# Quantised feed-forward on one core: block powers applied to clipped values, inverse by one integer operation, Silu and gated product 1024 wide

## The reference

```python
def _quantize_elem(x, ebits, mfrac, max_norm):
    ax = jnp.abs(x)
    priv = jnp.floor(jnp.log2(jnp.where(ax == 0, 1.0, ax)))
    priv = jnp.maximum(priv, float(-2 ** (ebits - 1) + 2))
    scale = jnp.exp2(priv - mfrac)
    return jnp.clip(jnp.round(x / scale) * scale, -max_norm, max_norm)

def _quantize_mx(x, ebits, mfrac, emax_elem, max_norm):     # blocks of 32 along the last axis
    amax = jnp.max(jnp.abs(xb), axis=-1, keepdims=True)
    sexp = jnp.floor(jnp.log2(jnp.where(amax == 0, 1.0, amax))) - emax_elem
    scale = jnp.exp2(jnp.clip(sexp, -127.0, 127.0))
    return _quantize_elem(xb / scale, ebits, mfrac, max_norm) * scale

def _mx_linear(x, w):                                       # activations: (2, 3, 2, 7.5); weights: (2, 1, 2, 6)
    return jnp.einsum('bsh,oh->bso', _q_act(x), _q_w(w))

inter = jax.nn.silu(_mx_linear(y, w_gate)) * _mx_linear(y, w_up)    # y = layernorm(x), 256 -> 1024
x = x + _mx_linear(inter, w_down)                                   # 1024 -> 256
```

## Time and profile before

| | |
|---|---|
| median of 3 runs | 835.02 us |
| lowest, highest | 833.01, 839.99 us |
| span of the profiled execution (first to last instruction) | 832.7 us |
| time of the profiled execution outside its span | not given; the lowest run is 0.3 above the span |
| feed-forward stage in the profile | from about 742 us to the end |
| busy over the span: PE, DVE, POOL, ACT | 90%, 74%, 69%, 49% |
| granted PE clock over the span | 0.986 of full speed |

### The profile page before, as it was taken

One profiled execution on the slowest core, in us unless ns is written; L12 is line 12 of the kernel. 1 busy time (PEld: TensorE's weight loads), 2 busy tenths in 40 slices (PEclk: granted clock), 3 DMA queues, 4 the chain that ended last, 5 costly groups with the idle time before them and its releaser, 6 DMA issues. The chain is left out here.

```text
span 832.7 us, 14911 instructions
## 1 busy us (share of the span) xinstructions
PE 750.6 (90%) x4808; PEld 535.8 (64%) x4808; DVE 615.8 (74%) x1115; ACT 406.6 (49%) x1084; POOL 570.9 (69%) x589
## 2 busy tenths in 40 slices
PE   4999999859999999689999999999999999866785
PEld 2555555447878877556777777777777777543454
DVE  5898999868887878665565576886678667749995
ACT  1688888533322322216454544555454445444453
POOL 5667776326676757564657778787878887716976
PEclk9999999989999999999999999999999999998999
DMA  9200000040000010122110000000000000000011
GB/s 262 103 1 0 0 0 1 2 168 20 20 19 20 19 57 0 57 95 96 48 49 1 1 1 1 3 1 1 1 1 2 1 2 1 1 2 7 25 33 38
DMA packets 8763, 24.12 MB, mean 29 GB/s; under 512 B 1711, under 2 KB 5167, under 8 KB 8087
## 3 DMA queue, kind: packets, MB, share of 16 engines
q1 hardware_dynamic: 8154, 23.28, 8.5%
q10 hardware_dynamic: 549, 0.08, 0.1%
HBM read 21.26 MB, written 2.10 MB: 28 GB/s over the span
## 5 line engine op out<-in xcount | busy, mean ns | idle before, releaser
L1606 POOL TENSOR_TENSOR q<-turned 64x512 f32<-64x512 f32 x128 | 168.0, 1313 | 23.5 <-DVE turned L1532 9.5
L1283 PE MATMUL ps<-l_yt,a 128*128 128x512 f32 x576 | 144.1, 400 | 2.1 <-ACT p L1429 1.6
L1283 PEld LDWEIGHTS ps<-l_yt,a 128*128 128x128 f32 x576 | 104.9, 188 | 26.9 <-issue 4.7
L1593 POOL TENSOR_TENSOR p<-p,l_inverse 128x512 f32<-128x512 f32 x64 | 66.8, 1047 | 77.3 <-DVE l_inverse L1554 76.9
L1429 ACT ACTIVATE p<-ps,l_negmax 128x128 f32<-128x128 f32 x256 | 91.1, 382 | 43.1 <-DVE l_negmax L1523 43.1
L1532 DVE TENSOR_TENSOR turned<-ps,rope 128x1024 f32<-128x1024 f32 x64 | 78.0, 1220 | 42.4 <-PE ps L1283 39.8
L871 PE MATMUL ps<-yt_experts,wsplit 128*128 (+1 forms) x384 | 97.3, 403 | 5.7 <-DVE h L974 5.2
L467 DVE TENSOR_REDUCE negmax<-ps 128x4 f32<-128x512 f32 x128 | 84.4, 685 | 13.3 <-PE ps L290 12.8
L871 PEld LDWEIGHTS ps<-yt_experts,wsplit 128*128 128x128 f32 x384 | 71.2, 192 | 23.1 <-issue 5.4
L1523 DVE TENSOR_REDUCE l_negmax<-ps 128x4 f32<-128x512 f32 x64 | 41.2, 686 | 45.8 <-PE ps L1341 45.6
L383 ACT ACTIVATE pt<-ps 128x512 f32<-128x512 f32 x128 | 71.2, 599 | 6.8 <-PE ps L312 4.5
(11 more groups left out here) (213 smaller groups left out, 1571.1 us busy)
## 6 DMA issues: line engine op xcount, KB each, us to landing
wide<-in_wide SPq DMA_DIRECT2D x8, 768.0 KB, 4.5
mx_raw<-in_mx SPq DMA_DIRECT2D x8, 384.0 KB, 3.1
x<-in_x SPq DMA_DIRECT2D x4, 512.0 KB, 8.4
ctx_t<-in_ctx_t SPq DMA_DIRECT2D x1, 2048.0 KB, 7.8
out<-x SPq DMA_DIRECT2D x16, 128.0 KB, 1.7
narrow<-in_narrow SPq DMA_DIRECT2D x8, 192.0 KB, 2.7
ktraw<-in_ctx_rows SPq DMA_DIRECT2D x1, 1248.0 KB
wraw<-in_gate SPq DMA_DIRECT2D x1, 1024.0 KB, 18.1
```

The source lines that it names most:

```text
L1283: out = pe.matmul(tile_bank(n, k), a[i][:, pa, kin, k * 128:(k + 1) * 128], yt[j % 2][:, py, kin, :, :].rearrange("p b s -> p (b s)"), sta ...
L1593: pool.tensor_tensor(p[:, head, :, :], p[:, head, :, :], spread(inverse[:, head, :], 2, S), ALU.mult).then_inc(normed[head], 1)
L1606: t = pool.tensor_tensor(out[rows[(head + half) % 2], head, :], turned[rows[head], half, :], turned[rows[head], 2 + half, :], ALU.add)
```

## The change

The block power that multiplies the clipped values is now the masked exponent itself, written straight to `hscale` in SBUF (L1913 of the changed kernel). Before it was 16 times that; the factor 16 (`PART`) moves to ACT's last copy of the down product (L1888), and the residual's identity is divided by 16 in a tensor of its own (`ident_part`, made once by POOL, L2005). The inverse is computed from the same bits by one integer operation, 250 x 2^23 minus the bits (L1914), in place of a scaling with a floor and a reciprocal. Silu and the gated product are one instruction of 1024 columns each, over two banks (L1872, L1899); `gated` is one buffer of 1024 in place of two of 512. PE makes the whole gate, then the whole up projection: gate waits for the Silu of the sequence before, up for its product.

```diff
-        gated = [sb(f"f_gated{i}", [S, 512]) for i in range(2)]
+        gated = sb("f_gated", [S, FFN])
...
+        ident_part = sb("f_ident_part", [128, 128])
-        gate_ps, up_ps = [m.ps[:, 0, :], m.ps[:, 2, :]], [m.ps[:, 1, :], m.ps[:, 3, :]]
+        gate_ps, up_ps = (m.ps[:, 2 * i:2 * i + 2, :].rearrange("s c n -> s (c n)") for i in range(2))
...
+        PART = 0.25 / UNIT
+        H_STEPS, INVERSE = 3, 250
...
-                    for half in range(2):
-                        wait(pe, h_made[half], n)
-                        for i, (bank, made) in enumerate(((gate_ps[half], gate_made[half]), (up_ps[half], up_made[half]))):
+                    for i, (banks, made, free) in enumerate(((gate_ps, gate_made, gated_made), (up_ps, up_made, h_made))):
+                        wait(pe, free, n)
+                        for half in range(2):
                             for k in range(HALVES):
                                 c = k * FFN + half * 512
-                                t = pe.matmul(bank, f.yqt[:, n, k * S:(k + 1) * S], m.wq[:, i, c:c + 512],
-                                              start=(k == 0), stop=(k == 1))
-                            t.then_inc(made, 1)
+                                t = pe.matmul(banks[:, half * 512:(half + 1) * 512], f.yqt[:, n, k * S:(k + 1) * S],
+                                              m.wq[:, i, c:c + 512], start=(k == 0), stop=(k == 1))
+                        t.then_inc(made, 1)
...
-                    pe.matmul(down_ps[par], m.ident[:, :], m.x[:, n - 4, :], start=True, stop=False)
+                    pe.matmul(down_ps[par], ident_part[:, :], m.x[:, n - 4, :], start=True, stop=False)
...
-                    for half in range(2):
-                        act.wait_ge(gate_made[half], n + 1)
-                        wait(act, h_made[half], n)
-                        act.activation(gated[half][:, :], gate_ps[half], ACT.Silu).then_inc(gated_made[half], 1)
+                    act.wait_ge(gate_made, n + 1)
+                    wait(act, h_made, n)
+                    act.activation(gated[:, :], gate_ps, ACT.Silu).then_inc(gated_made, 1)
...
-                    act.activation(m.x[:, n - 4, :], down_ps[par], ACT.Copy).then_inc(x_made, 1)
+                    act.activation(m.x[:, n - 4, :], down_ps[par], ACT.Copy, scale=PART).then_inc(x_made, 1)
...
-                dve.tensor_tensor(h[par][:, half * 512:(half + 1) * 512], gated[half][:, :], up_ps[half],
-                                  ALU.mult).then_inc(h_made[half], 1)
+                dve.tensor_tensor(h[par][:, :], gated[:, :], up_ps, ALU.mult).then_inc(h_made, 1)
...
-                then(2, dve.tensor_scalar(hmax[par].bitcast(U32), hmax[par].bitcast(U32), EXPONENT, None, ALU.bitwise_and))
                 wait(dve, hq_made, n - 3)
-                then(3, dve.tensor_scalar(hscale[place][:, :], hmax[par], 0.25 / UNIT, 2.0 ** -122 / UNIT,
-                                          ALU.mult, ALU.max))
-                then(4, dve.reciprocal(hinverse[par][:, :], hscale[place][:, :]))
+                bits = hscale[place][:, :].bitcast(U32)
+                then(2, dve.tensor_scalar(bits, hmax[par].bitcast(U32), EXPONENT, None, ALU.bitwise_and))
+                then(3, dve.tensor_scalar(hinverse[par][:, :].bitcast(U32), bits, -1.0, float(INVERSE << 23),
+                                          ALU.mult, ALU.add))
...
-                    combine(n, par, 0)
-                    combine(n, par, 1)
-                    dve.wait_ge(h_made[0], n + 1)
-                    dve.wait_ge(h_made[1], n + 1)
+                    combine(n, par)
+                    dve.wait_ge(h_made, n + 1)
...
+            pool.tensor_scalar(ident_part[:, :], m.ident[:, :], 1.0 / PART, None, ALU.mult).then_inc(part_made, 1)
             steps(pool, body)
```

More of the change, by code:

```diff
@@ L1783, in feed_forward @@
         half_ps = [h_ps[:, 0:512], m.bank(0).bitcast(BF16)[:, 0:512]]
-        gate_made, up_made, gated_made, h_made = (
-            [sem(f"f_{n}{i}") for i in range(2)] for n in ("gate_made", "up_made", "gated_made", "h_made"))
+        PART = 0.25 / UNIT
+        H_STEPS, INVERSE = 3, 250
+        gate_made, up_made, gated_made, h_made, part_made = (
+            sem(f"f_{n}") for n in ("gate_made", "up_made", "gated_made", "h_made", "part_made"))
         h_step, h8_made, hc_made, hq_made, hq_turned, hq_kept = (
@@ L1826, in body @@
                         pe.wait_ge(f.x_mid, GROUPS)
+                        pe.wait_ge(part_made, 1)
                     if n - 4 < B - 1:
@@ L1850, in turn_last @@
                 pe.wait_ge(hq_kept, B - 1)
-                pe.wait_ge(h_made[0], B)
+                pe.wait_ge(gated_made, B)
                 for half in range(2):
@@ L1890, in _, with combine @@
         def _(dve):
-            def combine(n, par, half):
-                dve.wait_ge(gated_made[half], n + 1)
-                dve.wait_ge(up_made[half], n + 1)
+            def combine(n, par):
+                dve.wait_ge(gated_made, n + 1)
+                dve.wait_ge(up_made, n + 1)
                 wait(dve, h8_made, n - 1)
-                dve.tensor_tensor(h[par][:, half * 512:(half + 1) * 512], gated[half][:, :], up_ps[half],
-                                  ALU.mult).then_inc(h_made[half], 1)
+                dve.tensor_tensor(h[par][:, :], gated[:, :], up_ps, ALU.mult).then_inc(h_made, 1)
             def scales_of_h(n, place):
@@ L1902, in then @@
                     instruction.then_inc(h_step, 1)
-                    dve.wait_ge(h_step, SCALE_STEPS * n + k)
+                    dve.wait_ge(h_step, H_STEPS * n + k)
                 par = place % 2
@@ L1981, in body @@
                 if inside(n, B):
-                    pool.wait_ge(h_step, SCALE_STEPS * (n + 1))
+                    pool.wait_ge(h_step, H_STEPS * (n + 1))
                     wait(pool, hc_made, n - 1)
```

## The result

| | before | after |
|---|---|---|
| median of 22 runs each | 833.88 us | 830.48 us |
| lowest, highest | 832.43, 844.25 | 827.94, 836.92 |
| span of the profiled execution | 832.7 | 828.5 |

The ratio of after to before is 0.9943, with a 95% interval of 0.9922 to 0.9963. That is 4.8 us of 833.9, and 3.1 to 6.5 by the interval; the two medians by themselves are 3.4 apart. Forecast were 4.8 less and a time of 830.2. The profiled execution of the changed kernel took 830.3 for a span of 828.5, so 1.8 lie outside its span. So about 0.3 of the gain lies where the profile doesn't show it, and comes with the wide form. The prediction had no term for it, and why it is so was not looked into.

A forecast was written before the change was run, and what follows sets the result against it. DVE, never idle in an undisturbed feed-forward step of 4.63, was taken as the bound. Steps 7.95 plus start 0.15 less holds 3.32 gave 4.78 saved: 835.0 - 4.8 = 830.2 us, range 825.8 to 835.0.

The forecast's parts named there:

- DVE sets the pace and POOL idles 0.85: Undisturbed feed-forward step of 4.63: DVE is never idle, POOL is free 3.86 after inverse ready and idles 0.85.
- Wide product, 0.13 a step: Gated product as one 1024-wide instruction: 0.06 saved by the merge, 0.07 by one wait less (0.06 to 0.13).
- Scales, 0.40 a step: Mask, scaling and reciprocal, 0.82 together, become two 32-wide instructions of 0.42 on DVE, saving 0.40 a step.
- The slow integer form: Integer inverse on DVE as slow as the reciprocal (0.35): 0.16 less saved a step, 2.4 less gain.
- Two holds: Steps 5 and 7: integer inverse held by POOL's third instruction to about 5.76, costing 1.66 each, 3.32 together.
- rival A: Integer inverse is not held, as its margin against POOL's third instruction is only 0.09: 827.4, chance 0.20.
- Start, 0.15 gained: Start of the feed-forward stage: with one-piece Silu the first inverse is ready at 747.22 against 747.37, gain 0.15.
- The rest at nothing: Single Silu buffer, whole-width waits, ACT's scaling, scaled identity, POOL's extra instruction cost nothing; Silu ready 0.2 early at group transposes.
- the 15 steps: Feed-forward stretch from first inverse ready to POOL's last divide; 7.95 saved over 15 intervals, less 3.32.
- B: PE at its low clock after waiting needs 7.3 a step and becomes the bound; 846.2, chance 0.07.
- the sign of B: In the changed profile, PE's granted clock below 1 after 775 was to mean B.
- C's closed ring: Single buffers close the ring of product, Silu and PE's queue at the old 4.63: 838.2, chance 0.07.

The follow-up runs named there:

- wide_only: Changed kernel with scales and reciprocal as before, so only Silu and gated product are 1024 wide; 833.32 us, ratio to before 0.9971, the 15 steps 71.48.
- scales_only: Kernel before with only the new scales, integer inverse and factor 16 in the last copy; 830.93 us, ratio to before 0.9935, the 15 steps 70.32.
- extra_psum: psum_const plus one full-width POOL product into an unread scratch tile at step 2; 835.96 us (1 run), the 15 steps 66.24.
- psum_const: Changed kernel with the integer inverse as scalar-tensor-tensor, adding a constant tile in PSUM; 827.65 us, ratio to before 0.9915, the 15 steps 65.81.
- pool_pause: Changed kernel plus a 1-wide POOL addition ahead of the last group's divide and its multiply; 828.28 us, ratio to before 0.9914, the 15 steps 67.40.
- after_again: Changed kernel profiled and timed again, no edit; 831.55 us, ratio to before 0.9941, the 15 steps 68.57.

## Why the prediction was right

Step by step, as it put them.

- DVE sets the pace and POOL idles 0.85: right. With DVE faster POOL's gap shrank to 0.31, and DVE still set the pace in every undisturbed step.
- Wide product, 0.13 a step: 0.135 by itself. Of the bounds, 0.06 to 0.13, the upper one held, since the gap of 0.10 did fall to 0.03. The reason given, one wait less, is not shown (see wide_only). The product itself went from 1.28 to 1.22, so the merge saved 0.06. The prediction's estimate by the Trainium skill (VectorE: DVE Perf Modes, The DRAIN you can't avoid, and the page's formula for a tensor-tensor instruction) was 0.16 for it, and the runs don't agree; the row was the better guide.
- Scales, 0.40 a step: scales_only shows 4.63 to 4.22, 0.41; the integer instruction is 0.18, not 0.19. The slow integer form, bound at 0.35, didn't come.
- Two holds, ending 5.76 after the inverse before: 5.77 and 5.77. At 4.09 undisturbed each costs 1.68; 1.66 was forecast. The margin of 0.09 that rival A turned on was 0.08 (769.31 to 769.39).
- Start, 0.15 gained: 0.14.
- The rest at nothing: Silu is 1.02 and hidden. At step 10 it is ready 0.06 ahead of the product (790.50 + 1.03 against 791.59) in the changed kernel, where I had 0.2. It cost nothing here and 0.32 in extra_psum.

The sum over the 15 steps: 15 x 0.54 = 8.10, less 2 x 1.68 = 3.36, and 0.20 for the interval of 4.83 in the profile before; together 4.94, and 4.95 was measured. Forecast were 4.63 for this part. No term of the sum was off by more than 0.15 over the 15 steps, and the missing 0.3 are 0.01 a step and that one interval, which the sum took for an undisturbed one.

The whole came out at 4.2 in the profiled spans and 3.1 to 6.5 in the runs. The closeness of the 830.48 to 830.2 is partly luck. The forecast started from 835.02, a median of 3 runs; that of 22 runs is 833.88, from which 4.8 less would be 829.1. And several parts that nobody forecast are as large as the terms: the 0.3 outside the span, the stage that began anywhere from 739 to 750 in ten profiled executions whose code ahead of it is the same, and the tail that is 1.7 longer when the clock falls in it. What is shown is the 15 steps. (The high end of the range, by its own terms, is 835.0 less 1.3 plus 1.6, that is 835.3 and not 835.0.)

The rivals. A, no hold, fell with the two long rows at 769.39 and 780.38. Its number for the 15 steps is what psum_const measured, 65.81, against 73.56 - 7.45 = 66.1 by its working. One sentence in it was wrong for the instruction as it is, that POOL would work off its backlog out of DVE's way: it does so with the form that is not held (psum_const), but in pool_pause the backlog met a request again and cost a hold. B, the low clock as the bound, didn't come in the 15 steps. The clock did fall after PE's wait at step 4, as PE's timeline of the changed kernel shows, four projections in 1.89 and then again in 1.04:

```profile
763.84 1.89 PE L1822 MATMUL ps<-wq,f_yqt 128*128 128x512 bf16 x4 [2.55 <-DVE f_h L1899]
...
774.83 1.04 PE L1822 MATMUL ps<-wq,f_yqt 128*128 128x512 bf16 x4 [2.44 <-DVE f_h L1899]
```

But the slack there hid it, and the almost equally long wait ahead of 774.83 brought no fall. A fall came at the end instead, where nothing hides it, and cost 1.7. The prediction named a clock below 1 after 775 as the sign of B. The sign appeared, 0.59 and 0.56 after 821, though not B, since PE bounded none of the 15 steps; the sign was drawn too wide, and the sum left the tail as it was. C's closed ring didn't come: the one place where DVE waited for Silu is the start.

## What to carry to other kernels

Before an instruction is replaced by a "cheaper" one, look at its form, not only at its length: here a tensor-scalar from SBUF to SBUF takes 0.18 when POOL is idle and up to the rest of POOL's running instruction when it isn't, and the time stands in its own duration, not as a wait. In a ring of two engines, work out at what offset the instruction asks and what the other engine is running at that offset, in the disturbed steps too. An operand in PSUM (a constant tile will do) kept the same arithmetic out of the conflict here for 5 ns.

## What was not expected of the hardware

- The hold ends with the POOL instruction that was running when the request came (782.66 + 1.66 = 784.32, the multiply's end being 784.29). It does so also where the next one is ready: in the earlier trace rows POOL's instructions follow each other, and the held 0.72 ends with the one that was running (531.31 against 531.30). In the feed-forward stage the next divide needs the very inverse that is held, so these holds alone don't tell.
- A 1-wide POOL instruction cost nothing: the inverse that asked 0.09 into it took 0.18. Whether it held the inverse for the 0.1 that it had left can't be seen, for that would end inside the 0.18.
- A reciprocal from SBUF to SBUF is not held (353 ns sixteen times, one of them 0.09 into a POOL instruction); a tensor-scalar of the same shape and place is, and so is a scalar-tensor-tensor with all operands in SBUF (0.56 or 1.68, in the kernel before).
- Behind two 512-wide products with a wait each the maximum starts 0.10 later, behind one of 1024 with one wait 0.03. What makes the 0.07 is open.
- The same kernel had PE's low level in its tail in one execution (0.59 and 0.56) and the full clock in another; after_again and the first profile have the same instructions up to there. What decides it is open.
